# A mixture-of-experts kernel whose largest slots travel through memory in the expert stage in place of at the end of routing

## The chip, the cores and the metric

The kernel runs on one core of one Trainium2 chip. The metric is device time in microseconds (us), of which each run has one; a kernel's figure is the median of its runs. A difference of about 0.3% is what the runs of this kernel can tell from no change. The engines are TensorE (PE), which multiplies, VectorE (DVE), ScalarE (ACT), GpSimd (POOL), which here issues gathers and scatters by index, and SyncE (SP), which here issues most of the other transfers.

## What is computed

Two transformer layers on 2048 tokens (4 sequences of 512) of width 256. Each layer adds an attention and a feed-forward block, both applied to the same layer norm. In the second layer the feed-forward block is a mixture of 64 experts:

```python
x = L0_attn_x
xn = _layernorm(x, axis=-1)
x = x + _L0_attn_ref(xn, ...) + _L0_ffn_ref(xn, ...)
xn = _layernorm(x, axis=-1)
x = x + _L1_attn_ref(xn, ...) + _L1_ffn_ref(xn, ...)

# in _L1_ffn_ref: 8 of 64 experts for each token
topk_idx = jax.lax.top_k(tmp, TOP_K)[1]
topk_w = jnp.take_along_axis(scores, topk_idx, axis=1)
topk_w = topk_w / (topk_w.sum(-1, keepdims=True) + 1e-20) * SCALE
w_full = w_full.at[jnp.arange(T)[:, None], topk_idx].add(topk_w)

def step(out, ws):
    wg, wu, wd, we = ws
    inter = jax.nn.silu(x @ wg.T) * (x @ wu.T)
    return (out + inter @ wd.T * we[:, None], None)
```

The second layer's attention runs over the batch of 4 sequences for each position, so it is small, and VectorE does it beside the experts.

## The kernel before

The program is a row of stages. Each is a block in which every engine has its own list of instructions, and an engine goes into the next stage only when all engines are through with this one (a barrier; its instructions carry the line of the stage's `with ctx`, L1158 or L1496). `layer0` and `layer1_front` take the first 620 us. The two stages of this case are `layer1_routing` and `layer1_experts`.

**Routing.** VectorE picks 8 experts for each token and gives each of the 16384 pairs of token and expert a slot. Slots are ordered by expert, each expert's share is padded to a multiple of 64 (`SEG`), and 128 slots make a block; there are 160 blocks (`NBLK`). One-hot products on TensorE invert this map. VectorE turns the result into `inv` (which token's row a slot takes, L1413) and `dst` (to which row of the memory tensor `y8` its result goes, L1419). GpSimd gathers the rows of blocks 0 and 1 as soon as `inv` is there (`ring.gather`, L189). SP loads experts 0 to 7 into the ring of 16 weight slots (`ring.load`, L183 and L185) and moves the tables of segments (`segments`, `segments_f`) from a column of 128 partitions into rows, through memory. ScalarE ends with a table load and a one-element activation (L1291).

**The largest slots.** The last stage wants to read 3 of each token's 8 results (`EARLY_ROWS`) before all are computed, and so has to know how many scatters must have landed. The slots of a token are sorted, `v8[:, :, TOPK - EARLY_ROWS]` is the largest that matters, and a reduce over the token tiles gives `latest`, one number on each of 128 partitions (L1382). SP stores this column to the memory tensor `latest` in pieces of 4 bytes (L1249), waits, and loads it back as one row on one partition (L1252). VectorE waits for the row (`be_moved` 128), takes its maximum and makes of it, in three further operations on one element, the semaphore value `scattered` (L1424 to L1428).

**Experts.** The blocks are pipelined over all engines. For block `j` GpSimd has gathered the rows into one of 8 buffers (blocks 2 to 9 at the start of this stage, L189, later ones when a buffer is free); TensorE transposes them (`e_ps_xT`, L1814) and VectorE copies them (`e_xT`, L1711); TensorE multiplies by gate and up weights (`e_ps_gu`, L1827), once for each half of 64 slots; ScalarE takes the silu (`e_sg`), VectorE multiplies (`e_h`, the gate, L1728), TensorE transposes (`e_ps_hT`, L1839), VectorE copies (`e_hT`), TensorE multiplies by the down weights (`e_ps_y`, L1850), ScalarE scales (`e_y`) and GpSimd scatters the rows into `y8` (L1633). TensorE takes the down product of block `j - 2` behind the gate and up product of block `j`. VectorE adds one step of the attention behind its work of each block (`attention(*part(j))`); block 100 has a step of the kind `k == 7`, the product `e_prod` at L1771. SP loads experts 8 to 63, each load once the last but one has landed (`landed(e - 1)`) and, from expert 16 on, once the slot is free. Behind all loads SP reads `scattered`, waits for so many scatters and for 12 results of the attention (`y1_ready`), and loads the early rows into `qkv1` (L1603). At the end SP loads the other rows tile by tile (L1613), VectorE adds up the even tiles (L1552), TensorE the odd ones (L1897).

Of the kernel before, what the change touches and what calls it, by code (L numbers as in the profile page):

```python
# [21 lines left out]
P = 128  # L22
# [1132 lines left out]
def layer1_routing(nc, t, late, ring, logits, xT, qkv1, seg_expert, expert_f, inv, dst, last, scattered):  # L1155

    ctx = ExitStack()
    with ctx:  # L1158
# [44 lines left out]
        spare = hi[:, :, :].rearrange("p x c -> p (x c)")  # L1203
        latest_row, latest, bound = spare[0:1, 0:P], spare[:, P:P + 1], spare[0:1, P + 1:P + 2]
# [19 lines left out]
        @block.sync  # L1224
        def _(sp):
            sp.wait_ge(zeroed, 1)
            sp.dma_start(t["rows"][TOK:TOK + P, :], zeros[:, :]).then_inc(cleared, 16)
            sp.wait_ge(w_ready, NT)
            sp.dma_start(t["rows"][0:TOK, D:ROW].rearrange("(n p) e -> p n e", p=P), w[:, :, :])\
              .then_inc(w_out, 16)  # L1230
            for e in range(ring.FIRST):
                ring.load(sp, t, e)

            sp.wait_ge(be_ready, 1)
            for r in range(2):
# [58 lines left out]
        def _(dve):  # L1294
# [87 lines left out]
            V.tensor_reduce(latest[:, :], v8[:, :, TOPK - EARLY_ROWS], AX.X, ALU.max).then_inc(pos_ready, 1)  # L1382
# [24 lines left out]
            for k in range(1, EIGHT):  # L1407
# [84 lines left out]
def layer1_experts(nc, t, ident, late, ring, x_sb, qkv1, seg_expert, expert_f, inv, dst, last, scattered):  # L1492
# [3 lines left out]
    with ctx:  # L1496
        NS, NW, NY, NQ = ring.NS, ring.NW, SCATTERS, 4
        LEAD, NF = 2, 5
        PAIRS = B * (B + 1) // 2
# [15 lines left out]
        mx = sbuf(ctx, nc, "e_mx", [P, H1])  # L1515
        y1 = sbuf(ctx, nc, "e_y1", [P, D])
# [22 lines left out]
        (early_in, summed, x_done_a, x_done_b, stored) = sems(  # L1539
            ctx, nc, "e_early_in", "e_summed", "e_x_done_a", "e_x_done_b", "e_stored")  # L1540
        y8_in = sems(ctx, nc, *(f"e_y8_in{f}" for f in range(NF)))

# [4 lines left out]
        def add_up(eng, E, i, ch, done):  # L1547

            f = i % NF
            eng.wait_ge(y8_in[f], (i // NF + 1) * 16)  # L1550
# [3 lines left out]
            if i in EARLY_TILES:  # L1554
                fold(EARLY_ROWS, qkv1[:, i, :])
                fold(1, y8[:, f, 4 * D:5 * D])
# [26 lines left out]
        def _(sp):  # L1583
# [6 lines left out]
            for e in range(ring.FIRST, NE):  # L1590
# [4 lines left out]
                landed(e - 1)  # L1595
            landed(NE - 1)

            first_rows = sp.value_load(scattered[0:1, 0:1], min_val=16, max_val=NBLK // NY * 16)
            for b in range(NY):
                sp.wait_ge(y_out[b], first_rows)  # L1600
            sp.wait_ge(y1_ready, EARLY_BATCHES * B)
            for i in EARLY_TILES:
                sp.dma_start(qkv1[:, i, :].rearrange("p (k d) -> p k d", d=D), rows8[i, :, LATER:TOPK, :])\  # L1603
# [101 lines left out]
        def _(dve):  # L1705
# [92 lines left out]
            dve.wait_ge(early_in, len(EARLY_TILES) * 16)  # L1798
# [9 lines left out]
        def _(pe):  # L1808
# [78 lines left out]
            pe.wait_ge(early_in, len(EARLY_TILES) * 16)  # L1887
            for i in range(1, NT, 2):
                f = i % NF
                pe.wait_ge(y8_in[f], (i // NF + 1) * 16)  # L1890
                if i // 2 >= 2:
                    pe.wait_ge(x_done_b, i // 2 - 1)
                for k in range(TOPK):
                    row = y8[:, f, k * D:(k + 1) * D]
                    if i in EARLY_TILES and k >= LATER:
                        row = qkv1[:, i, (k - LATER) * D:(k - LATER + 1) * D]
# [5 lines left out]
def kernel_program(nc, t):  # L1902
    ctx = ExitStack()
    with ctx:
# [12 lines left out]
        scattered = sbuf(ctx, nc, "scattered", [1, 1], I32)  # L1917
        layer1_front(nc, t, x_sb, yn, ident, late, ring.early_xT, ring.early_logits, qkv1)
        layer1_routing(nc, t, late, ring, ring.early_logits, ring.early_xT, qkv1, seg_expert, expert_f, inv, dst, last, scattered)
        layer1_experts(nc, t, ident, late, ring, x_sb, qkv1, seg_expert, expert_f, inv, dst, last, scattered)  # L1920
# [73 lines left out]
```

## Time and profile before

| | us |
|---|---|
| median of 3 runs | 1294.45 |
| lowest and highest run | 1294.40, 1297.47 |
| the profiled execution | 1291.48 |
| its span, first to last instruction | 1289.7 |

The span's own busy times, and the page's chain of work that ended last:

```profile
PE 1139.6 (88%) x7654; PEld 660.2 (51%) x7654; DVE 707.7 (55%) x2601; ACT 645.5 (50%) x1340; POOL 453.6 (35%) x525
PE 22%; issue 7%; another core or an unknown queue 6%; ACT 4%; DVE 3%; ACTq 2%; DMA 2%; DVEq 0%; POOL 0%; SPq 0%; POOLq 0%
```

The first line gives busy time, share of the span and number of instructions for each engine (PEld is TensorE's loading of weights, which overlaps its products). Engines whose name ends in q are the sequencers that issue for them; their times aren't in the busy times. A timeline row has the start, the duration, the engine, the line, the operation and `out<-in`, and in brackets how long the engine was idle before it and what ended that. The granted clock of TensorE is given as a share of 2.4 GHz.

### The profile page before, as it was taken

To read this page: it belongs to the slowest core of one execution; us is meant where nothing else is said; L and a number is where in the kernel's file an instruction comes from. 1 tells how busy PE (TensorE), PEld (TensorE's weight loads), DVE (VectorE), ACT (ScalarE), POOL (GpSimd) and SP (SyncE) were. 2 spreads that over 40 slices of the span, in tenths; PEclk is the share of its full clock that TensorE was granted. 3 is DMA by queue.
4 is the path that set the end of the run, shared out by engine and by line. 5 is a ranking of instruction groups with operands and counts; after the bars stand their busy time and mean duration, and the time that the engine had idled before them with its cause. 6 is when DMAs were issued, how large, how long until landed. Compare 5 with 4: busy or idle time off the path is not lost. (4 is left out here: it accounts for less than half of the span.)

```text
span 1289.7 us, 25449 instructions
## 1 busy us (share of the span) xinstructions
PE 1139.6 (88%) x7654; PEld 660.2 (51%) x7654; DVE 707.7 (55%) x2601; ACT 645.5 (50%) x1340; POOL 453.6 (35%) x525
## 2 busy tenths in 40 slices
PE   6679999999999999977974898988898889889967
PEld 3355666666666666455542444444444444444446
DVE  6576565666666666222882544454455455454536
ACT  4215454555555454634362565556555655565520
POOL 3333222222210000022003565565555555555520
PEclk9899999999999999999886999999999999999989
DMA  7401121121112110110066436526364334646248
GB/s 233 82 10 29 32 43 28 29 47 29 28 28 49 20 25 16 51 34 33 8 154 161 133 105 197 169 88 185 108 202 137 125 105 156 206 155 230 83 167 301
DMA packets 81682, 129.67 MB, mean 101 GB/s; under 512 B 32777, under 2 KB 53002, under 8 KB 81035
## 3 DMA queue, kind: packets, MB, share of 16 engines
q1 hardware_dynamic: 61576, 76.94, 21.2%
q0 software_dynamic: 15360, 47.21, 11.6%
q10 hardware_dynamic: 4616, 3.91, 1.0%
q8 instruction: 68, 1.11, 0.4%
q14 instruction: 62, 0.50, 0.1%
HBM read 97.57 MB, written 30.05 MB: 99 GB/s over the span
## 5 line engine op out<-in xcount | busy, mean ns | idle before, releaser
L684 DVE CUSTOM_DVE_ANT_0 a_masked<-a_ps_s,a_mask 128x512 bf16<-128x512 f32 (+3 forms) x512 | 230.0, 488 | 157.6 <-PE a_ps_s L843 153.8
L600 ACT ACTIVATE a_probs<-a_ps_e 128x512 f32<-128x512 f32 (+1 forms) x384 | 187.9, 526 | 120.1 <-PE a_ps_e L863 119.0
L1827 PE MATMUL e_ps_gu<-e_w_gu,e_xT 128*64 x640 | 227.3, 478 | 0.7 <-DVE e_xT L1711 0.7
L1827 PE MATMUL e_ps_gu<-e_s_gu,e_xT 128*64 128x352 f32 x640 | 227.3, 478 | 0.0
L1633 POOL DMA_INDIRECT y<-e_y,dst x160 | 160.4, 1002 | 185.4 <-ACT e_y L1657 81.2
L1850 PE MATMUL e_ps_y<-e_w_d,e_hT 88*64 x640 | 169.8, 388 | 52.8 <-DVE e_hT L1736 37.7
L189 POOL DMA_INDIRECT yn<-rows,inv x160 | 158.3, 989 | 123.8 <-DVE inv L1413 61.4
L1850 PE MATMUL e_ps_y<-e_s_d,e_hT 88*64 88x256 f32 x640 | 170.2, 388 | 0.0
L1728 DVE TENSOR_TENSOR e_h<-e_sg,e_ps_gu 128x176 f32<-128x176 f32 x160 | 54.0, 338 | 211.2 <-ACT e_sg L1648 120.7
L1850 PEld LDWEIGHTS e_ps_y<-e_w_d,e_hT 88*64 88x64 f32 x640 | 81.7, 137 | 148.1 <-issue 124.5
L860 PE MATMUL a_ps_e<-a_qT,a_kT 75*128 75x512 bf16 (+3 forms) x512 | 140.8, 303 | 2.1 <-ACT a_probs L600 1.8
L843 PE MATMUL a_ps_s<-a_kT,a_qT 72*128 72x512 bf16 (+3 forms) x512 | 130.9, 300 | 11.7 <-DVE a_headmax L684 11.4
L1666 ACT ACTIVATE e_s_gu<-e_w_gu 128x704 f32 x160 | 125.2, 783 | 11.6 <-SPq L1586 11.5
L919 PE MATMUL a_ps_f<-a_xnT,a_w_gu 128*128 128x256 f32 x512 | 125.5, 388 | 5.6 <-DVE a_hT L709 3.2
L1648 ACT ACTIVATE e_sg<-e_ps_gu 128x176 f32<-128x176 f32 x160 | 50.0, 312 | 153.1 <-remote 107.1
L1827 PEld LDWEIGHTS e_ps_gu<-e_w_gu,e_xT 128*64 128x64 f32 x640 | 75.4, 138 | 83.2 <-issue 83.2
L1657 ACT ACTIVATE e_y<-e_ps_y,e_weight 128x256 f32<-128x256 f32 x160 | 75.4, 471 | 76.0 <-PE e_ps_y L1850 63.3
L863 PE MATMUL a_ps_e<-a_causal,a_identb 128*128 128x128 bf16 x512 | 112.3, 220 | 0.0
L919 PEld LDWEIGHTS a_ps_f<-a_xnT,a_w_gu 128*128 128x128 f32 x512 | 93.6, 192 | 22.8 <-DVE a_hT L709 10.8
L456 POOL CAST a_m_parts<-a_negmaxT 32x128 bf16<-32x128 f32 x16 | 4.5, 279 | 275.6 <-DVE a_negmaxT L727 155.0
L1671 ACT ACTIVATE e_s_d<-e_w_d 88x512 f32 x160 | 98.9, 618 | 0.0
L1711 DVE COPY e_xT<-e_ps_xT 128x256 f32<-128x256 f32 x160 | 67.7, 423 | 49.8 <-PE e_ps_xT L1814 42.4
(235 smaller groups left out, 1902.6 us busy)
## 6 DMA issues: line engine op xcount, KB each, us to landing
e_w_gu<-e_gu SPq DMA_DIRECT2D x64, 352.0 KB
e_w_d<-e_down SPq DMA_DIRECT2D x64, 176.0 KB
a_qT<-qk_parts SPq DMA_DIRECT2D x48, 192.0 KB
e_w_gu<-y SPq DMA_DIRECT2D x12, 640.0 KB, 6.5
qkv<-y SPq DMA_DIRECT2D x12, 384.0 KB
qk_parts<-a_stage SPq DMA_DIRECT2D x16, 256.0 KB, 2.6
e_w_gu<-y SPq DMA_DIRECT2D x4, 1024.0 KB, 7.0
yn<-rows,inv POOLq DMA_INDIRECT x160
```

What stands on the lines that cost most here:

```text
L189: eng.indirect_dma_start(self.x[:, j % self.NS, :], None, t["rows"], bass.IndirectOffsetOnAxis(inv[:, j:j + 1], 0)).then_inc(self.x_in[j % ...
L600: nc.scalar.activation(probs[:, i % HKV, UCOL[u]:UCOL[u + 1]], ps_e[:, (i * 3 + u) % 2, 0:w], ACT.Exp, scale=SCALE0).then_inc(exp_done, 1)
L684: ins = V.tensor_tensor_reduce(masked[:, n % 2, c:c + w], ps_s[:, n % 2, c:c + w], mask[:, T - w:T], 1.0, -3e38, ALU.add, ALU.max, headmax ...
L843: ins = nc.tensor.matmul(ps_s[:, x % 2, c:c + (a + 1) * P], qT[0:MROW, n % NQ, g, a * P:(a + 1) * P], kT[0:MROW, b % 2, g, 0:(a + 1) * P], ...
L860: nc.tensor.matmul(ps_e[:, x % 2, c:c + T - a * P], kT[:, b % 2, g, a * P:(a + 1) * P], qT[:, n % NQ, g, a * P:T], start=True, stop=False, ...
L863: ins = nc.tensor.matmul(ps_e[:, x % 2, c:c + P], identb[:, :], causal[:, :], start=False, stop=True, skip_group_check=True)
L919: ins = nc.tensor.matmul(ps_f[:, w * HALF:(w + 1) * HALF], w_gu[:, k, w, i * P:(i + 1) * P], xnT[:, n % NX, k, :], start=(k == 0), stop=(k ...
L1633: pool.indirect_dma_start(t["y8"], bass.IndirectOffsetOnAxis(dst[:, j:j + 1], 0), y[:, j % NY, :], None).then_inc(y_out[j % NY], 16)
L1666: nc.scalar.activation(s_gu[:, j % 2].rearrange("p k i -> p (k i)"), w_gu[:, bass.ds(expert & (NW - 1), 1), :, :].rearrange("p a k i -> p ...
L1671: nc.scalar.activation(s_d[:, j % 2].rearrange("p k d -> p (k d)"), w_d[0:HI1, bass.ds(expert & (NW - 1), 1), :, :].rearrange("p a k d -> ...
L1827: ins = nc.tensor.matmul(ps_gu[r * SEG:(r + 1) * SEG, j % 2, 0:2 * INTER1], xT[:, j % 2, k * P + r * SEG:k * P + (r + 1) * SEG], w.rearran ...
L1850: ins = nc.tensor.matmul(ps_y[r * SEG:(r + 1) * SEG, 0:D], hT[:, j % 2, k * P + r * SEG:k * P + (r + 1) * SEG], w.rearrange("p a d -> p (a ...
```

## The change

The store of `latest`, the load back and the four operations leave the routing stage. The column now stays in a tile of its own, `latest_slot`, into the expert stage. There SP stores it behind load 9 (`e == ring.FIRST + 1`), and behind load 15 (`e == NW - 1`) waits for the store and loads the row into an unused part of `seg_expert`. VectorE waits for the row behind its attention step of block 100 and does the four operations there. SP reads `scattered` after its wait for `y1_ready`, not before. The semaphore `early_in` is gone: the store, the load back and the early rows count on the first semaphore of the last part's tiles (`y8_in[0]`), so VectorE and TensorE wait for the early rows and the first tile together. A new tile `e_bound` of 4 bytes lies ahead of `e_y1` and `e_yT`. The slices `early8` and `LATER - 4` are what `qkv1[:, i, :]` and 1 were, with `EARLY_ROWS` = 3.

```diff
 def layer1_routing(...)
         @block.sync
             sp.wait_ge(be_moved, 96)
-
-            sp.wait_ge(pos_ready, 2)
-            sp.dma_start(t["latest"].rearrange("(p a) -> p a", a=1), latest[:, :],
-                         allow_slow_non_contiguous=True).then_inc(be_moved, 16)
-            sp.wait_ge(be_moved, 112)
-            sp.dma_start(latest_row[:, :], t["latest"].rearrange("(a p) -> a p", a=1)).then_inc(be_moved, 16)
-            sp.wait_ge(be_moved, 128)
         @block.vector
-            V.tensor_reduce(latest[:, :], v8[:, :, TOPK - EARLY_ROWS], AX.X, ALU.max).then_inc(pos_ready, 1)
+            ch.did(V.tensor_reduce(latest[:, :], v8[:, :, TOPK - EARLY_ROWS], AX.X, ALU.max))
...
-            dve.wait_ge(be_moved, 128)
-            ch.step(V.tensor_reduce(bound[:, :], latest_row[:, :], AX.X, ALU.max))
-            ch.step(V.tensor_scalar(bound[:, :], bound[:, :], -1.0 - CHOSEN - (SCATTERS * P - 1) / 2,
-                                    1.0 / (SCATTERS * P), ALU.add, ALU.mult))
-            ch.step(V.tensor_scalar(bound[:, :], bound[:, :], 2.0 ** 23, None, ALU.add))
-            ch.step(V.tensor_scalar(scattered[:, :], bound[:, :], 1.0 - 2.0 ** 23, 16.0, ALU.add, ALU.mult))
 def layer1_experts(...)
+        FIRST_ROWS_AT = 100
+        bound = sbuf(ctx, nc, "e_bound", [1, 1])
+        early8 = qkv1[:, :, 3 * D - EARLY_ROWS * D:3 * D]
+        spare = seg_expert[0:1, 3 * P:4 * P].bitcast(F32)
+        scattered = seg_expert[0:1, 3 * P - 1:3 * P]
+        early_in, EARLY_COUNT = y8_in[0], 32 + len(EARLY_TILES) * 16
+
+        def landed_y8(i):
+
+            return y8_in[i % NF], (i // NF + 1) * 16 + (0 if i % NF else EARLY_COUNT)
         @block.sync
                 ring.load(sp, t, e)
                 landed(e - 1)
+                if e == ring.FIRST + 1:
+                    sp.dma_start(t["latest"].rearrange("(p a) -> p a", a=1), latest[:, :],
+                                 allow_slow_non_contiguous=True).then_inc(early_in, 16)
+                if e == NW - 1:
+                    sp.wait_ge(early_in, 16)
+                    sp.dma_start(spare, t["latest"].rearrange("(a p) -> a p", a=1)).then_inc(early_in, 16)
             landed(NE - 1)
-            first_rows = sp.value_load(scattered[0:1, 0:1], min_val=16, max_val=NBLK // NY * 16)
+            sp.wait_ge(y1_ready, EARLY_BATCHES * B)
+            first_rows = sp.value_load(scattered, min_val=16, max_val=NBLK // NY * 16)
             for b in range(NY):
                 sp.wait_ge(y_out[b], first_rows)
-            sp.wait_ge(y1_ready, EARLY_BATCHES * B)
         @block.vector
                 if j < NBLK:
                     attention(*part(j))
-            dve.wait_ge(early_in, len(EARLY_TILES) * 16)
+                if j == FIRST_ROWS_AT:
+
+                    dve.wait_ge(early_in, 32)
+                    ch.step(V.tensor_reduce(bound[:, :], spare, AX.X, ALU.max))
+                    ch.step(V.tensor_scalar(bound[:, :], bound[:, :], -1.0 - CHOSEN - (SCATTERS * P - 1) / 2,
+                                            1.0 / (SCATTERS * P), ALU.add, ALU.mult))
+                    ch.step(V.tensor_scalar(bound[:, :], bound[:, :], 2.0 ** 23, None, ALU.add))
+                    ch.step(V.tensor_scalar(scattered, bound[:, :], 1.0 - 2.0 ** 23, 16.0, ALU.add, ALU.mult))
+            dve.wait_ge(early_in, EARLY_COUNT + 16)
         @block.tensor
-            pe.wait_ge(early_in, len(EARLY_TILES) * 16)
+            pe.wait_ge(early_in, EARLY_COUNT + 16)
             for i in range(1, NT, 2):
                 f = i % NF
-                pe.wait_ge(y8_in[f], (i // NF + 1) * 16)
+                pe.wait_ge(*landed_y8(i))
```

## Rows read from the trace of the kernel before

**Rows 1.** Waits in 670 to 705 us: waiter, releaser, total, times, longest.

```profile
DVE d_hi L1424 <- DMA d_hi<-latest: 11.4, 1, 11.4
```

**Rows 2.** Timeline, 676 to 695 us: the stages' border.

```profile
677.10 0.35 SPq L1249 DMA_DIRECT2D latest<-d_hi  x1
...
677.73 0.95 POOL L189 DMA_INDIRECT yn<-rows,inv  x1 [0.30 <-issue]
678.90 0.20 ACT L1291 ACTIVATE d_warm<-l_bias 128x1 f32<-128x1 f32 x1
684.97 0.24 SPq L1252 DMA_DIRECT2D d_hi<-latest  x1
687.73 0.27 DVE L1424 TENSOR_REDUCE d_hi<-d_hi 1x1 f32<-1x128 f32 x1 [11.37 <-DMA d_hi<-latest]
...
688.39 0.14 DVE L1428 TENSOR_SCALAR scattered<-d_hi 1x1 int32<-1x1 f32 x1
...
689.09 0.66 PE L1814 MATMUL e_ps_xT<-ident_sb,yn 128*128 128x128 f32 x2 [12.35 <-PEq L1158]
...
689.69 0.94 POOL L189 DMA_INDIRECT yn<-rows,inv  x1 [11.01 <-POOLq L1158]
...
690.93 0.94 POOL L189 DMA_INDIRECT yn<-rows,inv  x1 [0.30 <-issue]
...
694.00 0.34 SPq L183 DMA_DIRECT2D e_w_gu<-e_gu  x1
...
694.29 0.29 PEld L1814 LDWEIGHTS e_ps_xT<-ident_sb,yn 128*128 128x128 f32 x2 [1.08 <-DMA yn<-rows,inv]
```

**Rows 3.** The chain that ended last, 640 to 760 us: start, duration, what.

```profile
690.93 5.79 DMA yn<-rows,inv
...
703.92 0.62 PE e_ps_xT L1814 x2
```

**Rows 4.** DMA queues in 678 to 679, 678.5 to 679, 680.5 to 685.5 us: packets, MB, share.

```profile
q0 software_dynamic: 47, 0.16, 55.9%
...
q1 hardware_dynamic: 119, 0.00, 13.4%
...
DMA packets 21, 0.05 MB, mean 10 GB/s; under 512 B 11, under 2 KB 11, under 8 KB 21
```

**Rows 5.** DMA packets in 666 to 668 us, and SP's timeline around them.

```profile
DMA packets 791, 0.12 MB, mean 60 GB/s; under 512 B 736, under 2 KB 736, under 8 KB 791
...
654.70 3.05 SPq L1238 DMA_DIRECT2D segments_f<-d_be  x1
673.62 0.25 SPq L1241 DMA_DIRECT2D seg_expert<-segments  x1
```

**Rows 6.** Gates of L1728 up to 1038.90 us; timeline, 1038.9 to 1043.4 us, block 100.

```profile
694.00:1038.90 344.90, 34.10 (x101) 0.98 0.48 149
...
1038.98 0.68 DVE L1771 TENSOR_TENSOR e_prod<-qkv,e_e 128x512 f32<-128x512 f32 x1
...
1040.22 0.34 DVE L1728 TENSOR_TENSOR e_h<-e_sg,e_ps_gu 128x176 f32<-128x176 f32 x1 [0.56 <-DVE e_prod L1771]
...
1043.31 0.23 PEld L1839 LDWEIGHTS e_ps_hT<-ident_sb,e_h 128*88 128x88 f32 x2
```

**Rows 7.** Timeline, 1248 to 1251 us: the first two tiles of rows.

```profile
1248.57 0.96 DVE L1552 TENSOR_TENSOR e_w_gu<-e_w_gu,qkv 128x768 f32<-128x768 f32 x1 [8.88 <-DMA e_w_gu<-y]
...
1250.41 1.19 PE L1897 MATMUL e_ps_gu<-e_w_gu,ident_sb 128*128 128x256 f32 x2 [9.49 <-DMA e_w_gu<-y]
```

**Rows 8.** Stretches: length, busy PE, PEld, DVE, ACT, POOL; clock; DMA share; GB/s.

```profile
676.74:681.50 4.76, 0.00 (x0) 0.00 (x0) 0.00 (x0) 2.30 (x3) 1.64 (x2) 1.00 0.66 58
681.50:689.06 7.56, 0.00 (x0) 0.00 (x1) 0.70 (x4) 0.00 (x0) 0.00 (x0) 0.50 0.05 7
689.06:695.00 5.94, 4.57 (x16) 1.74 (x18) 1.29 (x5) 2.06 (x4) 4.09 (x5) 0.50 0.73 223
...
701.00:709.00 8.00, 7.05 (x28) 3.19 (x28) 3.26 (x13) 2.46 (x6) 1.97 (x2) 0.57 0.73 217
```

More of the change, by code:

```diff
@@ L1152, in _, with layer1_routing @@
             router(NT - 1)
-def layer1_routing(nc, t, late, ring, logits, xT, qkv1, seg_expert, expert_f, inv, dst, last, scattered):
+def layer1_routing(nc, t, late, ring, logits, xT, qkv1, seg_expert, expert_f, inv, dst, last, latest):
     ctx = ExitStack()
@@ L1202, in layer1_routing @@
         none = sbuf(ctx, nc, "d_none", [P, P], FP16)
-        spare = hi[:, :, :].rearrange("p x c -> p (x c)")
-        latest_row, latest, bound = spare[0:1, 0:P], spare[:, P:P + 1], spare[0:1, P + 1:P + 2]
         ps_inv = psum(ctx, nc, "d_ps_inv", [P, 4, 512])
@@ L1489, in _, with layer1_experts @@
                 qkv(n, 1)
-def layer1_experts(nc, t, ident, late, ring, x_sb, qkv1, seg_expert, expert_f, inv, dst, last, scattered):
+def layer1_experts(nc, t, ident, late, ring, x_sb, qkv1, seg_expert, expert_f, inv, dst, last, latest):
     ctx = ExitStack()
@@ L1538, in layer1_experts @@
         rows8 = t["y8"][0:TOK * TOPK].rearrange("(i p k) d -> i p k d", p=P, k=TOPK)
-        (early_in, summed, x_done_a, x_done_b, stored) = sems(
-            ctx, nc, "e_early_in", "e_summed", "e_x_done_a", "e_x_done_b", "e_stored")
+        early8 = qkv1[:, :, 3 * D - EARLY_ROWS * D:3 * D]
+        spare = seg_expert[0:1, 3 * P:4 * P].bitcast(F32)
+        scattered = seg_expert[0:1, 3 * P - 1:3 * P]
+        (summed, x_done_a, x_done_b, stored) = sems(
+            ctx, nc, "e_summed", "e_x_done_a", "e_x_done_b", "e_stored")
         y8_in = sems(ctx, nc, *(f"e_y8_in{f}" for f in range(NF)))
+        early_in, EARLY_COUNT = y8_in[0], 32 + len(EARLY_TILES) * 16
+        def landed_y8(i):
+            return y8_in[i % NF], (i // NF + 1) * 16 + (0 if i % NF else EARLY_COUNT)
         def done_of(i):
@@ L1549, in add_up @@
             f = i % NF
-            eng.wait_ge(y8_in[f], (i // NF + 1) * 16)
+            eng.wait_ge(*landed_y8(i))
             def fold(n, other):
@@ L1554, in add_up @@
             if i in EARLY_TILES:
-                fold(EARLY_ROWS, qkv1[:, i, :])
-                fold(1, y8[:, f, 4 * D:5 * D])
+                fold(EARLY_ROWS, early8[:, i, :])
+                fold(LATER - 4, y8[:, f, 4 * D:LATER * D])
             else:
@@ L1595, in _ @@
                 landed(e - 1)
+                if e == ring.FIRST + 1:
[4 more added lines that the diff above has]
+                    sp.dma_start(spare, t["latest"].rearrange("(a p) -> a p", a=1)).then_inc(early_in, 16)
             landed(NE - 1)
-            first_rows = sp.value_load(scattered[0:1, 0:1], min_val=16, max_val=NBLK // NY * 16)
+            sp.wait_ge(y1_ready, EARLY_BATCHES * B)
+            first_rows = sp.value_load(scattered, min_val=16, max_val=NBLK // NY * 16)
             for b in range(NY):
                 sp.wait_ge(y_out[b], first_rows)
-            sp.wait_ge(y1_ready, EARLY_BATCHES * B)
             for i in EARLY_TILES:
-                sp.dma_start(qkv1[:, i, :].rearrange("p (k d) -> p k d", d=D), rows8[i, :, LATER:TOPK, :])\
+                sp.dma_start(early8[:, i, :].rearrange("p (k d) -> p k d", d=D), rows8[i, :, LATER:TOPK, :])\
                   .then_inc(early_in, 16)
@@ L1895, in _ @@
                     if i in EARLY_TILES and k >= LATER:
-                        row = qkv1[:, i, (k - LATER) * D:(k - LATER + 1) * D]
+                        row = early8[:, i, (k - LATER) * D:(k - LATER + 1) * D]
                     ins = nc.tensor.matmul(ps_gu[:, i // 2 % 2, 0:D], ident[:, :], row,
@@ L1916, in kernel_program @@
         last = sbuf(ctx, nc, "last", [1, NE], I32)
-        scattered = sbuf(ctx, nc, "scattered", [1, 1], I32)
+        latest = sbuf(ctx, nc, "latest_slot", [P, 1])
         layer1_front(nc, t, x_sb, yn, ident, late, ring.early_xT, ring.early_logits, qkv1)
-        layer1_routing(nc, t, late, ring, ring.early_logits, ring.early_xT, qkv1, seg_expert, expert_f, inv, dst, last, scattered)
-        layer1_experts(nc, t, ident, late, ring, x_sb, qkv1, seg_expert, expert_f, inv, dst, last, scattered)
+        layer1_routing(nc, t, late, ring, ring.early_logits, ring.early_xT, qkv1, seg_expert, expert_f, inv, dst, last, latest)
+        layer1_experts(nc, t, ident, late, ring, x_sb, qkv1, seg_expert, expert_f, inv, dst, last, latest)
 def constants():
```

## The prediction

> **What bounds the kernel now.** The page comes first: TensorE is the busiest engine, and in the expert stage the others work for it, so a stretch without TensorE is time lost. The edit sits where the routing stage ends and the expert stage begins; the waits from 670 to 705 us [rows 1] show VectorE idle for 11.4 us there, on a DMA that writes `d_hi` from `latest`. The timeline of the same stretch [rows 2] gives the order, and the reader should follow the engines to the barrier between the stages one by one. VectorE ends `dst` at 687.73 - 11.37 = 676.36 and has nothing until 687.73; its last operation ends at 688.39 + 0.14 = 688.53, and TensorE starts the expert stage at 689.09. So one chain sets the end of routing: the store of `latest` (issued 677.10), its landing, the load back (issued 684.97, used from 687.73) and four operations on one element.
>
> **What the others have done by then** [rows 2]. SP is past its wait for `expert_f` at 677.10, where it issues the store. GpSimd's second gather ends at 677.73 + 0.95 = 678.68. ScalarE ends its warm-up at 678.90 + 0.20 = 679.10. TensorE has done nothing since 676.74 [rows 8]. Without the chain ScalarE is last.
>
> **Part 1: the chain leaves the end of routing.** Out of it go two DMAs, their waits on SP, one wait and four operations on VectorE. The last arrival moves from 688.53 to 679.10: 9.43 us. What follows the barrier keeps its distance to it: TensorE 689.09 - 688.53 = 0.56 us, GpSimd 689.69 - 688.53 = 1.16 us [rows 2]. The chain of work that ended last [rows 3] goes from the barrier over GpSimd's gathers for blocks 2 and 3 to a landing at 690.93 + 5.79 = 696.72 and on into TensorE, so it moves by the same 9.43 us. The blocks follow no clock of their own, so the shift is kept to the end unless something below gives it back. Term: -9.4 us.
>
> **Part 2: gathers 0 and 1 lose their cover.** Now they have 10 us to land before TensorE wants them. Gather 2 ends on GpSimd at 689.69 + 0.94 = 690.63, and TensorE, which waits for it, starts at 694.29: 3.66 us. Gather 3 ends at 691.87 and lands at 696.72: 4.85 us. Both have two expert loads beside them [rows 2, 3]. Gather 0 ends at 677.73 - 0.30 = 677.43, gather 1 at 678.68; by 3.66 us they land at 681.1 and 682.3, by 4.85 us at 682.3 and 683.5. Shifted by 9.43, TensorE wants them at 689.09 - 9.43 = 679.7 and, one transpose and copy later, at about 680.9. So it starts up to 2.6 us late. It then has under 4.6 us of work (689.06 to 695.00, at the low clock [rows 8]) before it needs gather 3, at 696.72 - 9.43 = 687.3: 682.3 + 4.6 = 686.9. Hidden; I take 0, with 0 to 2.6 us as bounds.
>
> **Part 3: the store of `latest` in its new place.** It is issued after expert load 9, once load 8 has landed. That is where load 10 goes out now, at 694.00 [rows 2], so the store is issued at about 684.6, and load 10 behind it on SP and in queue 1 about 0.4 us later. SP's wait for it comes after load 15, when everything up to load 14 has landed, so SP isn't held. The cost is another one. The store is 128 pieces of 4 bytes. Of its packets 119 run in 678.5 to 679, and it lands at 684.97. Queue 0, which moved gather 0 (0.16 MB) in 678 to 679, puts only 21 packets, at 10 GB/s, into 680.5 to 685.5: the tail of gather 1, issued just behind the store [rows 4]. There is a second case: `segments` and `segments_f`, also in 4 byte pieces, have their last packets in 666 to 668, and SP can go on only at 673.62 [rows 5]. I read both as: such a store is confirmed some 5.5 us after its last packet, and transfers of other queues on the same DMA engines stall meanwhile. In the new place gather 3 and later and load 10 are what can stall. Load 10 doesn't matter, since experts 0 to 8 are there. Gather 3 does. It lands at 687.3 and its last packets move about 1 us before, at 686.3. The store's packets come at 684.6 + 1.4 = 686.0 at the earliest (677.10 to 678.5 now), and behind what is left of load 9. That is a near miss. If gather 3 is caught, it lands at about 686.5 + 5.5 = 692.0 and costs 4.7 us. If it isn't, gather 4 is caught, but that is wanted only at 703.92 - 9.43 = 694.5 [rows 3]. I take 0, the time order being for it, with 0 to 4.7 us as bounds.
>
> The Trainium skill (DMA: Bandwidth & Descriptors, Queues, rings and completion order) says that the increment of a semaphore lands only after every earlier write of that DMA engine, of all its queues. By that rule alone the store was confirmed late because gather 1 was slow; it would delay nobody, and the term would be 0 with no bound above. The second case speaks against it as the whole story, for no gather was under way there.
>
> **Part 4: the load back and the four operations.** The load (684.97 to 687.73 with its landing) goes behind load 15, and nobody wants it before block 100. VectorE has made 101 gates (`e_h`) by 1038.90, so its step of block 100 is the one at 1038.98 [rows 6]. The four operations take 688.53 - 687.73 = 0.80 us there. Queued behind them is the gate of block 101, with 0.56 us of idle time in front of it, so it is pushed by 0.3 us, and the copies of `e_xT` and `e_hT` behind it by no more. TensorE transposes this `e_h` at 1043.31; the gate ends at 1040.56: 2.7 us of cover. Term 0; 0.8 us without the cover.
>
> **Part 5: what else is touched.** The reduce into `latest` is the same operation on another tile. SP reads `scattered` after its wait for `y1_ready` in place of before; both stand behind all 64 expert loads, so 0. At the end VectorE and TensorE wait for the first tile of rows together with the early ones. VectorE waited for it anyway (until 1248.57), and TensorE starts at 1250.41, later than that [rows 7]: 0. `e_bound` moves the tiles behind it by 4 bytes; no row prices that, and I put it at 0 with the 0.3 us of block 100 as bound on either side.
>
> **Part 6: TensorE's clock.** It was granted 1.00 (2.4 GHz) until 681.50, 4.8 us after the last matmul, 0.50 (1.2 GHz) from there to 695.00, and 0.57 on average from 701 to 709 [rows 8]. After the change TensorE restarts at about 681, so the first dip may stay away, but what it slows is waiting for gather 3 anyway. The second dip lies on the path: 7.05 us of matmuls at 0.57 would be 4.0 us at 1.00, so it costs 3.0 us. It may go, or another may come with a changed rhythm: -3.0 to +3.0, taken as 0.
>
> **The sum.** -9.43 + 0 (gathers 0, 1) + 0 (store) + 0 (block 100) + 0 (clock) = -9.4 us. The profiled execution took 1291.48 us (span 1289.7), so its like would take 1282.1. The median of the runs before is 1294.45, 3.0 us above it, and what is compared is medians: 1294.45 - 9.4 = 1285.0 us.
>
> **Rivals.** (a) Gather 3 is caught by the store: 9.4 - 4.7 = 4.7 us gained, 1289.7 us. For it speaks the crawl of gather 1; against it load 9 ahead of the store and gather 3's head start. (b) The forecast with the second clock dip gone: 9.4 + 3.0 = 12.4, 1282.0 us. For it speaks that TensorE's long rest at the low clock goes; against it that the idle time just before 701 stays. (c) Nothing moves: the barrier, or code behind it, is late for another reason. Only the crowd of waiting engines speaks for it; against it each engine's last work is seen, at 679.10 or before. 1294.5 us. (d) Slower. One mechanism: the store takes as long behind loads as `segments_f` did, 654.70 to 673.62 = 18.9 us from its issue [rows 5], and holds gather 3 all that time: 684.6 + 18.9 = 703.5 against 687.3 costs 16.2 us, net +6.8, 1301.3 us. From a landing of gather 3 after 696.7 on it is slower. Against it: `segments_f` had most of eight loads ahead, the store has at most one.
>
> **Chances.** Forecast 0.54 (1282.5 to 1287.5 around 1285.0), (a) 0.26 (1288 to 1292), (b) 0.10, (c) 0.06, (d) 0.04. A measurement of this kernel tells 0.3%, 3.9 us, from no change. Faster by more: 0.54 + 0.10 + two thirds of (a) = 0.82. Within: the rest of (a) and (c) = 0.14. Slower 0.04. For 8 in 10 the range takes the forecast, (b) but for its end, and two thirds of (a), up to 1290.5: 1280.0 to 1290.5.
>
> **What would show it.** Right: VectorE has no wait behind `dst`; ScalarE's warm-up is the last work before TensorE's first transpose, 0.5 to 3 us before it; TensorE's wait for gather 3 ends about 9.4 us earlier; the four operations stand behind block 100's step, and TensorE's next transpose of `e_h` doesn't wait for VectorE. Queue 0 crawls for about 5 us after the store's packets if my reading of them holds. Rival (a): gather 3's wait ends only 4 to 5 us earlier. The forecast is wrong if a gather, from block 3 on, holds TensorE longer than now, or if a shift that is there at block 10 is gone at block 150.

## The result and the profile after

| | before | after |
|---|---|---|
| median, 8 runs each, us | 1297.18 | 1285.91 |
| lowest and highest, us | 1291.44, 1300.21 | 1284.40, 1290.04 |
| profiled execution: time, span | 1291.48, 1289.7 | 1285.63, 1283.8 |

The ratio is 0.9924, with a 95% interval of 0.9903 to 0.9946: 9.9 us of 1297.18, between 7.0 and 12.6; the two medians as they stand differ by 11.3. Run again beside other kernels (`after_again`), the changed kernel came to 0.9939 (0.9913 to 0.9965).

The changed kernel's timeline at the border of the stages, which answers to [rows 2]. Columns are as there.

```profile
677.88 0.38 DVE L1404 SCALAR_TENSOR_TENSOR inv<-d_is_pad,l_ids,d_token 128x160 uint32<-128x160 f32 x1
...
679.05 0.33 DVE L1410 SCALAR_TENSOR_TENSOR dst<-d_row,d_pad_row 128x160 uint32<-128x160 f32 x1
679.20 1.24 POOL L189 DMA_INDIRECT yn<-rows,inv  x1 [62.06 <-DVE inv L1404]
...
680.74 0.95 POOL L189 DMA_INDIRECT yn<-rows,inv  x1 [0.30 <-issue]
681.91 0.20 ACT L1282 ACTIVATE d_warm<-l_bias 128x1 f32<-128x1 f32 x1
684.06 0.66 PE L1821 MATMUL e_ps_xT<-ident_sb,yn 128*128 128x128 f32 x2 [4.31 <-PEq L1158]
...
684.65 0.94 POOL L189 DMA_INDIRECT yn<-rows,inv  x1 [2.96 <-POOLq L1158]
...
688.91 0.34 SPq L1590 DMA_DIRECT2D latest<-latest_slot  x1
```

VectorE has nothing behind `dst`: the wait of [rows 1] is gone. But the two spans can't be laid on each other by their clocks. `inv`, which the edit doesn't touch, begins at 677.88, where it began at 674.87 before:

```profile
674.87 0.38 DVE L1413 SCALAR_TENSOR_TENSOR inv<-d_is_pad,l_ids,d_token 128x160 uint32<-128x160 f32 x1
```

Of these 3.0 us, 1.2 are seen at 200 us already, in stages whose code is the same, and 2.35 at the reduce into `latest` (645.85 before, 648.20 after), which is the first operation that the edit touches. The rest is no effect of the edit that could be told: from this reduce to `inv` the kernels below take 28.1 to 29.7 us, though the code between the two is the same in nearly all of them. So I count from `inv` on, in this kernel and in all others below. "The barrier opens" is read from TensorE's first transpose of the expert stage:

| us after `inv` begins | before | after | moved |
|---|---|---|---|
| TensorE's first transpose of the expert stage | 14.22 | 6.18 | 8.0 |
| gate (`e_h`) of block 0 | 19.88 | 11.84 | 8.0 |
| gate of block 5 | 39.78 | 28.10 | 11.7 |
| gate of block 50 | 192.44 | 182.49 | 10.0 |
| gate of block 99 | 359.09 | 348.35 | 10.7 |
| gate of block 159, the last | 561.51 | 552.47 | 9.0 |
| end of the span | 614.83 | 605.92 | 8.9 |

The border gives 8.0 us, the first blocks some 3.6 more, the long stage gives back 2.7, and 8.9 us are left, which with the 3.0 us of drift makes the 5.9 us between the spans. Only the first three rows can be leaned on. In `after_again`, with the same code, they are 6.14, 11.81 and 28.05, within 0.1 us of this execution; but the gate of block 99 comes at 351.87 there, 3.5 us later than here. So a difference of 2 or 3 us deep in the long stage can't be told from what one execution differs from the next.

### The profile page after: what moved, and what is told of

Same layout as the page of the kernel before. It is cut to its first block and busy times, and to the rows that moved or that the text cites. A ratio compares the mean times of both kernels' runs of the same rounds, so it can differ in the third digit from the quotient of the medians.

```text
span 1283.8 us, 25448 instructions
## 1 busy us (share of the span) xinstructions
PE 1143.0 (89%) x7654; PEld 660.1 (51%) x7654; DVE 707.9 (55%) x2601; ACT 645.6 (50%) x1340; POOL 456.3 (36%) x525
## 5 line engine op out<-in xcount | busy, mean ns | idle before, releaser
L1834 PE MATMUL e_ps_gu<-e_w_gu,e_xT 128*64 x640 | 230.3, 483 | 0.7 <-DVE e_xT L1710 0.7
L1834 PE MATMUL e_ps_gu<-e_s_gu,e_xT 128*64 128x352 f32 x640 | 230.3, 483 | 0.0
L1632 POOL DMA_INDIRECT y<-e_y,dst x160 | 163.0, 1019 | 181.8 <-ACT e_y L1656 85.0
```

Of the source, the lines that this page charges most:

```text
L1632: pool.indirect_dma_start(t["y8"], bass.IndirectOffsetOnAxis(dst[:, j:j + 1], 0), y[:, j % NY, :], None).then_inc(y_out[j % NY], 16)
L1834: ins = nc.tensor.matmul(ps_gu[r * SEG:(r + 1) * SEG, j % 2, 0:2 * INTER1], xT[:, j % 2, k * P + r * SEG:k * P + (r + 1) * SEG], w.rearran ...
```

## The experiments

Each compares with the kernel before on the same chip, timed in 5 rounds or, where no ratio is given, in one profiled execution. The edits are against the changed kernel where nothing else is said. On the chip of the second set (three stores, row store, late store, row made on TensorE) the kernel before was slower, 1302.15 us against 1294.18 and 1294.48 in the other two, so only ratios, and times counted from `inv` near the border, go across the sets.

### No transport at all

```diff
-                if e == ring.FIRST + 1:
-                    sp.dma_start(t["latest"]..., latest[:, :], ...).then_inc(early_in, 16)
-                if e == NW - 1:
-                    ...
-                if j == FIRST_ROWS_AT:
-                    ...
-            first_rows = sp.value_load(scattered, ...)
             for b in range(NY):
-                sp.wait_ge(y_out[b], first_rows)
+                sp.wait_ge(y_out[b], 256)
```

> Nothing of the largest slots travels: no store, no load back, no operations at block 100; SP waits for a constant number of scatters (256 on each of the eight semaphores, worked out beforehand from the routing) in place of the computed one. Theory A (the stalled DMA engines cost nothing that TensorE sees): time as the changed kernel's, ratio to before 0.990 to 0.993; the packets of the gathers in the 8 us behind load 9 move at more than 100 GB/s. Theory B (the stalls reach TensorE through gather 3 or a later one): 4 to 5 us less than the changed kernel, ratio 0.988 or 0.989.

Beside the two transfers, VectorE's four operations at block 100 are left out. Measured: 0.994 (0.9913 to 0.9967), so what the changed kernel still does for the slots costs nothing that these runs can tell. But the DMA engines do feel it. The same 8 us, from 16 us after `inv` on, in the changed kernel and in this one (length; busy time and count of PE, PEld, DVE, ACT, POOL; granted clock, DMA share, GB/s), the changed kernel first:

```profile
693.88:701.88 8.00, 7.63 (x48) 3.69 (x48) 3.96 (x17) 4.13 (x9) 2.44 (x3) 0.88 0.79 64
```

```profile
691.90:699.90 8.00, 5.14 (x28) 2.52 (x28) 3.58 (x15) 3.85 (x8) 2.35 (x3) 0.79 0.95 282
```

With the store 64 GB/s move, without it 282. `after_again`, the changed kernel in another execution, has the crawl for 6 us, from 15 to 21 us after `inv`:

```profile
689.99:695.99 6.00, 3.50 (x26) 1.63 (x26) 2.67 (x11) 2.73 (x6) 1.26 (x3) 1.00 0.72 75
```

So its length isn't fixed: here 6 us, above about 8. TensorE is busy for 7.63 of 8 us in the first fence, so it isn't starved there; but that it is busier than in the second (5.14) is no effect of the store, for in the same stretch of `after_again` it is 5.50. Theory A holds: the rate is above 100 GB/s, and the ratio lies nearer to its range (0.990 to 0.993) than to that of B, though the interval excludes neither a small cost nor a small gain.

### The store put back, with nobody waiting for it

```diff
 # routing, SP, behind its wait for expert_f
+            sp.wait_ge(pos_ready, 2)
+            sp.dma_start(t["latest"].rearrange("(p a) -> p a", a=1), latest[:, :],
+                         allow_slow_non_contiguous=True).then_inc(ring.latest_in, 16)
 # experts, SP
-                if e == ring.FIRST + 1:
-                    sp.dma_start(...)
```

> The store goes back to the end of routing, but nobody waits for it there; load back and operations stay in the expert stage. Theory A (a store in 4 byte pieces stalls the DMA engines for 5.5 us and more, and what is queued behind it with them): the barrier opens as in the changed kernel, about 6.2 us after inv, but gather 1 lands only about 10 us after inv, so TensorE transposes block 1 about 4 us later than the changed kernel does, counted from inv; ratio to before about 0.996. Theory B (a store's confirmation only waits for earlier writes and delays nobody): block 1 is transposed 1.3 us after block 0, ratio 0.992.

The timeline of this kernel at the border, with `inv` at 680.53:

```profile
680.45 0.34 SPq L1248 DMA_DIRECT2D latest<-latest_slot  x1
...
683.39 0.95 POOL L190 DMA_INDIRECT yn<-rows,inv  x1 [0.30 <-issue]
684.56 0.20 ACT L1287 ACTIVATE d_warm<-l_bias 128x1 f32<-128x1 f32 x1
...
692.00 0.66 PE L1823 MATMUL e_ps_xT<-ident_sb,yn 128*128 128x128 f32 x2 [9.60 <-PEq L1159]
...
692.60 0.94 POOL L190 DMA_INDIRECT yn<-rows,inv  x1 [8.25 <-POOLq L1159]
```

And its stretch from 4 to 10 us after `inv`, in the columns of the last two fences:

```profile
684.53:690.53 6.00, 0.00 (x0) 0.00 (x0) 0.00 (x0) 0.22 (x2) 0.00 (x0) 0.71 0.39 29
```

Every engine's last work before the barrier is over at 684.76, nobody waits for the store, and yet TensorE starts at 692.00: 11.47 us after `inv` at 680.53, against 6.18 in the changed kernel. In the last fence the gathers trickle at 29 GB/s; their last packets fall between 10 and 11 us after `inv`. The ratio is 1.0005 (0.9979 to 1.0031): nearly all of the gain is gone. I had expected 0.996; the 2.75 us that the border is still ahead of the kernel before would be 0.998, at the edge of the interval. (The last gate of this one profile, 554.15 us after `inv`, would promise far more: it can't be trusted for such sums.) This refutes that a store delays nobody. In one respect it went otherwise than I expected: I foresaw block 1's transpose to be late and the barrier to be on time, and it is the barrier that is late, with GpSimd's queue the one that has gathers under way. That SP is held there by its own store, still unconfirmed, is a rival that no run here excludes for this kernel and for the one with two such stores below; what speaks for GpSimd stands in the next section.

### Who is last at the barrier

```diff
 # e_one_gather
-    NS, NW, SOON, FIRST = 8, 16, 2, 8
+    NS, NW, SOON, FIRST = 8, 16, 1, 8
 # e_no_table
-            nc.scalar.activation(warm[:, :], late.bias[:, 0:1], ACT.Silu)
```

> Gather 1 moves behind the barrier. In the changed kernel TensorE's first transpose of the expert stage begins 6.18 us after inv begins and 1.95 us after ScalarE's last work. Theory G (GpSimd goes through the barrier only when its gathers are out, one gather costing 1.2 us): the first transpose begins about 5 us after inv. Theory S (ScalarE's table load is last): still 6.2 us. Theory C (the code behind the barrier): still 6.2 us.

> ScalarE's table load and one-element activation are left out at the end of routing, so the table load falls to the first silu of the expert stage. Theory S (ScalarE is last at the barrier): the first transpose begins about 1.5 us earlier, 4.7 us after inv. Theories G (GpSimd last) and C (code behind the barrier): still 6.2 us.

With one gather (first fence) and without the table load (second):

```profile
683.47 0.20 ACT L1282 ACTIVATE d_warm<-l_bias 128x1 f32<-128x1 f32 x1
...
684.36 0.41 PE L1821 MATMUL e_ps_xT<-ident_sb,yn 128*128 128x128 f32 x2 [3.06 <-PEq L1158]
...
684.96 0.96 POOL L189 DMA_INDIRECT yn<-rows,inv  x1 [2.96 <-POOLq L1158]
...
689.68 0.69 PE L1821 MATMUL e_ps_xT<-ident_sb,yn 128*128 128x128 f32 x2 [4.91 <-DMA yn<-rows,inv]
```

```profile
680.45 0.96 POOL L189 DMA_INDIRECT yn<-rows,inv  x1 [0.30 <-issue]
683.79 0.41 PE L1820 MATMUL e_ps_xT<-ident_sb,yn 128*128 128x128 f32 x2 [4.33 <-PEq L1158]
```

One gather less in the routing stage opens the barrier 4.92 us after `inv` (684.36 - 679.44) in place of 6.18. Without the table load it opens at 6.20 (683.79 - 677.59), as before. So ScalarE, which I had taken, isn't last in the changed kernel, and GpSimd is. With one gather the two may be level: ScalarE's last work ends 4.23 us after `inv` (683.67 - 679.44), and in the kernel before the first transpose followed the last arrival by 0.56 us, so the gather may cost a little more than the 1.26 us seen.

These two runs don't tell issuing a gather (1.25 us each) from its being out, for both are taken away at once. The packets do. Over five kernels the last packets of GpSimd's queue fall into the half microsecond that begins, counted from `inv`, at 4.0 (one gather), 5.0 (changed kernel), 5.0 (row store in the whole chain, below), 10.5 (store put back) and 13.0 (two stores, below), and TensorE's first transpose comes at 4.92, 6.18, 6.16, 11.47 and 13.89, each time 0.4 to 1.2 us behind them. GpSimd had issued its last gather by 3.8 us after `inv` in all five. So the barrier follows the landing. In the kernel before, the last packets fall at 10.0 to 10.5 and the transpose at 14.22: there the gathers too are late, behind the chain that is later still. The gain of one gather less is no use by itself: gather 1 then starts late, and TensorE waits 4.91 us for it.

### More stores, another store, another place

```diff
 # e_three_stores, on top of e_nothing
+                if ring.FIRST + 1 <= e <= ring.FIRST + 3:
+                    n = e - ring.FIRST - 1
+                    sp.dma_start(t["latest"][n * P:(n + 1) * P].rearrange("(p a) -> p a", a=1), latest[:, :], ...)
 # e_row_store, on top of e_nothing
+                if e == ring.FIRST + 1:
+                    sp.dma_start(t["latest"].rearrange("(a p) -> a p", a=1), seg_expert[0:1, 0:P].bitcast(F32))
 # e_store_later
-                if e == ring.FIRST + 1:
+                if e == 24:
-                if e == NW - 1:
+                if e == 32:
```

> As the kernel in which nothing travels (SP waits for the constant 256), but with three stores of the column in 4 byte pieces, behind loads 9, 10 and 11. Theory A (each such store stalls the DMA engines some 5.5 us or more): gathers 4 to 9 land late enough to hold TensorE, blocks 3 to 8 come 5 to 12 us later than in the changed kernel, ratio to before 0.995 to 1.001. Theory B (a store delays nobody): as with no store, 0.990 to 0.993, and the packets behind the stores move at more than 100 GB/s.

> As the kernel in which nothing travels (SP waits for the constant 256), but with one store of 512 bytes in one piece (a row of another tile) where the changed kernel stores the column. Theory A (the 4 byte pieces are what stalls): no crawl, the gathers' packets in the 8 us behind it move at more than 100 GB/s. Theory B (any store to memory between the loads does): the same crawl as in the changed kernel, at 15 to 70 GB/s.

> The store goes behind load 24 and the load back behind load 32. Theory A (4 byte pieces stall the DMA engines wherever they are): no crawl at the start of the stage, and one of the same kind, 5 us and more with less than 100 GB/s, behind load 24; TensorE isn't held, since gathers run several blocks ahead there. Theory B (the crawl belongs to the start of the stage, with its eight gathers and loads at once): the crawl stays at the start.

SP's timeline with three stores, then the 8 us from 16 us after `inv` on with the row store, then, for the late store (issued at 797.20, behind load 24), one stretch that is nearly all ahead of it and two behind it:

```profile
687.43 0.34 SPq L1591 DMA_DIRECT2D latest<-latest_slot  x1
687.81 0.43 SPq L183 DMA_DIRECT2D e_w_gu<-e_gu  x1
688.28 1.82 SPq L185 DMA_DIRECT2D e_w_d<-e_down  x1
698.14 0.34 SPq L1591 DMA_DIRECT2D latest<-latest_slot  x1
```

```profile
694.46:702.46 8.00, 4.34 (x22) 2.01 (x20) 3.17 (x13) 3.42 (x7) 1.60 (x3) 0.79 0.79 255
```

```profile
790.00:798.00 8.00, 7.68 (x51) 3.49 (x49) 3.35 (x12) 4.56 (x10) 4.80 (x5) 1.00 0.85 259
...
802.00:803.00 1.00, 1.00 (x11) 0.47 (x9) 0.96 (x2) 0.32 (x1) 0.70 (x2) 1.00 0.87 39
...
804.00:806.00 2.00, 1.65 (x15) 0.65 (x10) 1.66 (x3) 0.82 (x2) 1.69 (x2) 1.00 0.99 63
```

With three stores SP waits from 690.10 to 698.14 before it can go on, where without a store it issues a load about every 3 us; with the changed kernel's one store the like wait is 6.1 us (693.56 to 699.71). With one piece of 512 bytes there is no crawl (255 GB/s). With the store behind load 24 the crawl is there, at 39 to 70 GB/s for some 6 us, and TensorE is busy through it. So the crawl belongs to the 4 byte pieces, and to no place. The ratio of three stores is 0.9944 (0.9918 to 0.997): I had expected 0.995 or more under theory A, with blocks 3 to 8 late by 5 to 12 us. The gate of block 5 comes 34.32 us after `inv`, where it comes at 31.01 and 32.58 in the two kernels without such stores on the same chip (row made on TensorE, row store), and the one of block 10 at 50.18 against 47.27 and 48.74: 1.4 to 3.3 us late. So even so much stalling hardly reaches TensorE.

### The row made on TensorE

```diff
+                if j == FIRST_ROWS_AT - 4:
+                    nc.tensor.transpose(ps_yT[0:1, D:D + P], latest[:, :], ident[:, :]).then_inc(row_ready, 1)
...
-                    dve.wait_ge(early_in, 32)
-                    ch.step(V.tensor_reduce(bound[:, :], spare, AX.X, ALU.max))
+                    dve.wait_ge(row_ready, 1)
+                    ch.step(V.tensor_reduce(bound[:, :], ps_yT[0:1, D:D + P], AX.X, ALU.max))
```

> The column becomes a row on TensorE: one transpose at block 96 into unused columns of the PSUM bank of e_ps_yT, read there by VectorE's reduce at block 100; no store, no load back. Theory A (the stalls cost nothing that TensorE sees): as the changed kernel, ratio to before 0.990 to 0.993. Theory B (they do): 4 to 5 us less, 0.988 or 0.989. Under both it isn't slower than the changed kernel: one transpose of about 0.3 us is added among 160 blocks.

0.9926 (0.9896 to 0.9956): as the changed kernel, with no DMA for the slots at all. It doesn't beat it.

### The changed kernel again, beside the last set

> The changed kernel once more, beside the others of this set on the same chip: ratio to before 0.990 to 0.995.

0.9939 (0.9913 to 0.9965): the gain is there in another set of runs too.

### Must the chain leave the routing stage?

```diff
 # e_chain_with_row_store, on top of the kernel before
-            sp.dma_start(t["latest"].rearrange("(p a) -> p a", a=1), latest[:, :],
-                         allow_slow_non_contiguous=True).then_inc(be_moved, 16)
+            sp.dma_start(t["latest"].rearrange("(a p) -> a p", a=1),
+                         seg_expert[0:1, 0:P].bitcast(F32)).then_inc(be_moved, 16)
 # e_store_with_segments, on top of the kernel before: the same store, issued right behind segments_f
-            sp.wait_ge(be_moved, 48)
+            sp.wait_ge(pos_ready, 2)
+            sp.dma_start(t["latest"]..., latest[:, :], ...).then_inc(be_moved, 16)
+            sp.wait_ge(be_moved, 64)
+            sp.dma_start(latest_row[:, :], ...).then_inc(be_moved, 16)
 # e_two_stores_at_end, on top of e_store_at_end_of_routing
+            for n in range(2):
```

> The kernel before with its whole chain at the end of routing, but with a store of 512 bytes in one piece (a row of another tile) in place of the column, so that the number that is worked out is not that of the slots, and SP waits for the constant 256 in its place. Theory A (the 4 byte pieces are what is slow): the store is confirmed in 2 to 3 us in place of 7.9, VectorE's last operation ends 8 to 9 us after inv in place of 13.7, and the first transpose begins 9 us after inv in place of 14.2. Theory B (any store and load back costs this): nothing moves.

> The kernel before, with the store of the column issued together with segments and segments_f, some 20 us earlier, and the load back with theirs; all of it and the four operations stay in the routing stage. Theory A (the gain comes from having no store in 4 byte pieces, and no wait for one, near the border of the stages; where the rest is done doesn't matter): VectorE doesn't wait, its four operations end about 2.4 us after inv, the first transpose begins 6.2 us after inv, and the ratio is that of the changed kernel, 0.990 to 0.995. Theory B (the expert stage is the only place where it is hidden): the wait stays in part, ratio 0.996 to 1.000.

> As the kernel with the unwaited store at the end of routing, with two such stores one behind the other. Theory A1 (a stall has a length of its own for each piece): the tail of gather 1 and the barrier with it come 4 to 6 us later than with one store, the first transpose 16 to 17 us after inv. Theory A2 (the length is that of one confirmation, however many pieces are on the way): within 1.5 us of one store, 11.5 to 13 us after inv.

The timeline of the whole chain, with a row in place of the column:

```profile
677.49 0.39 DVE L1413 SCALAR_TENSOR_TENSOR inv<-d_is_pad,l_ids,d_token 128x160 uint32<-128x160 f32 x1
...
678.64 0.24 SPq L1249 DMA_DIRECT2D latest<-seg_expert  x1
...
679.73 0.22 SPq L1252 DMA_DIRECT2D d_hi<-latest  x1
...
681.67 0.14 DVE L1428 TENSOR_SCALAR scattered<-d_hi 1x1 int32<-1x1 f32 x1
...
683.65 0.41 PE L1813 MATMUL e_ps_xT<-ident_sb,yn 128*128 128x128 f32 x2 [4.29 <-PEq L1158]
```

The number that it makes isn't that of the slots, and SP waits for the constant 256. The store is on its way for 1.1 us (678.64 to 679.73) where the column took 7.9. VectorE is through 4.3 us after `inv`, and the barrier opens at 6.16, exactly as with the whole chain moved away. I had expected 9. One execution took 1283.96 us, less than any of the 23 of the kernel before on this chip (lowest 1289.99). So the move isn't what helps at the border: the pieces are. With them gone, both the wait and the crawl of the gathers that holds GpSimd are gone.

The store issued early, with `segments`, was a miss for theory A. It isn't free there. Issued at 659.99, behind the pieces of `segments` and `segments_f`, it lets SP go on with the load back only 2.8 us after `inv` (680.24). In the kernel before, SP went on with `seg_expert` 1.3 us before `inv` [rows 5], in the kernel with the store put back 3.5 us before it. So the tables that it is queued with come 4 us later or more, and VectorE waits for them:

```profile
681.52 0.20 ACT L1288 ACTIVATE d_warm<-l_bias 128x1 f32<-128x1 f32 x1
684.24 0.27 DVE L1421 TENSOR_REDUCE d_hi<-d_hi 1x1 f32<-1x128 f32 x1 [5.26 <-DMA expert_f<-segments_f]
```

The wait is for `expert_f`, through the count that it shares. The barrier opens at 8.10 and the ratio is 0.9975 (0.9951 to 0.9999). Two stores at the end open the barrier 13.89 us after `inv` (693.33 - 679.44), 2.4 us more than one. Neither A1 (4 to 6) nor A2 (under 1.5) foretold that; how the stall grows with the number of pieces stays open, and each of the two is one execution.

## Why the prediction was right, and where its steps were not

**The sum** was -9.4 us and 1285.0 us; the median is 1285.91, the ratio says -9.9 (-7.0 to -12.6). Sign and size hold. That 1285.0 is within 1 us of the median is in part luck: it starts from 1294.45, the median of 3 runs before, and with 8 runs that is 1297.18. The one term in the sum was 1.4 us too large, and the 8.0 us that were measured for it lie in the interval by themselves; that something else made up for the rest isn't shown. (In the chances a sum is off by 0.01: 0.54 + 0.10 + two thirds of 0.26 is 0.81.)

**Part 1, the border.** The mechanism is shown: the chain was last, and without it the barrier opens sooner. The size is 8.0 us and not 9.43, and the step that failed is "Without the chain ScalarE is last". I had read GpSimd's last work off the end of its issuing (678.68). It goes through the barrier when its gathers have landed; the runs with one gather and without the table load, and the last packets in five kernels, show it. My sign for this step, ScalarE's warm-up as the last work 0.5 to 3 us before the first transpose, came true (1.95 us) and told nothing: it can't tell ScalarE from a queue whose end isn't on the engine's timeline. Of the 8.0 us, taking away the waits alone gives 2.75 (14.22 to 11.47, store still there), and only the absence of the column's pieces gives the other 5.3 (11.47 to 6.18). The other way round, with the pieces away and the waits kept, all 8.1 are there (14.22 to 6.16). What the pieces do I had not in the sum's reasoning at all, though the crawl of gather 1 stood in [rows 4].

**Part 2, gathers 0 and 1.** I had put their lateness at 0 to 2.6 us behind the barrier. It is in the barrier: 1.4 us of it (9.43 against 8.0), and behind it block 1 is transposed 1.3 us after block 0, with no wait for a gather. The 3.66 and 4.85 us that I took for a gather's landing were too long for these two, which have no loads beside them: in the changed kernel the last packets of gather 1 are through by 683.4, 1.7 us after its issue ends (681.69). And the 3.66 us was an upper bound only. I had read "TensorE, which waits for it, starts at 694.29" off the row of a weight load; TensorE's products before it run to 694.35 in the profile, so gather 2 may have landed well before.

**Part 3, the store.** My reading of the two cases was right, and the rule of the Trainium skill (DMA: Bandwidth & Descriptors, Queues, rings and completion order), that a confirmation waits for the earlier writes of its engine, isn't the whole story: in `e_store_at_end_of_routing` the gathers crawl behind a store that nobody waits for. The stall is longer than my 5.5 us (8 us at 64 GB/s, and 6 us at 75 in `after_again`). Gather 3 wasn't caught, as forecast. The waits at the start of the stage in the changed kernel (waiter, releaser, total, times, longest):

```profile
PE e_ps_xT L1821 <- PEq L1158: 4.3, 1, 4.3
...
PEld e_ps_xT L1821 <- DMA yn<-rows,inv: 3.3, 2, 2.2
```

The longer of the two waits in there, for gather 2, ends at 690.37, and most of the store's pieces move from 690.9 to 691.9, where 119 packets under 512 bytes go, after 39 in the microsecond before. The shorter, for gather 3, is one of TensorE's weight load and hidden: gather 3 didn't gate. TensorE took it at 693.53, straight out of block 1's matmuls, which ran at the low clock: 15.65 us after `inv` against 21.90, which is 6.2 us of shift, less than the 9.4 that I had expected for it. Gather 2 lands 5.7 us after its issue begins here and 4.6 us in the kernel without transport, but 4.6 us too with three stores, of which the first goes out at the same place, and in `after_again`, whose code is the same. So the 1.1 us is a difference between executions and not the store's.

**Part 4, block 100.** Shown, on VectorE's timeline of the changed kernel:

```profile
1031.94 0.68 DVE L1770 TENSOR_TENSOR e_prod<-qkv,e_e 128x512 f32<-128x512 f32 x1
1032.65 0.27 DVE L1800 TENSOR_REDUCE e_bound<-seg_expert 1x1 f32<-1x128 f32 x1
...
1033.31 0.14 DVE L1804 TENSOR_SCALAR seg_expert<-e_bound 1x1 int32<-1x1 f32 x1
1033.49 0.34 DVE L1727 TENSOR_TENSOR e_h<-e_sg,e_ps_gu 128x176 f32<-128x176 f32 x1
```

From 1032.65 to 1033.45 they take 0.80 us, as foreseen, and the gate of block 101 follows 2.67 us after the one of block 100, where it followed after 2.36 in the kernel before, 0.3 us less. But its rhythm around block 100 was another. The kernel without transport has the changed kernel's rhythm there, and not the operations; its gates of blocks 100 and 101:

```profile
1031.58 0.34 DVE L1720 TENSOR_TENSOR e_h<-e_sg,e_ps_gu 128x176 f32<-128x176 f32 x1 [1.55 <-ACT e_sg L1640]
1033.41 0.34 DVE L1720 TENSOR_TENSOR e_h<-e_sg,e_ps_gu 128x176 f32<-128x176 f32 x1
```

They are 1.83 us apart. So the gate is pushed by the whole 0.8 us and not by 0.3, and the cover holds all the same: the gate of block 102 follows the one of block 99 after 11.25 us with the operations and 11.22 without. The term 0 is right. The ratio without them is no better either (0.994).

**Part 5.** Nothing speaks against its zeros: from the last gate to the end of the span it is 53.32 us before and 53.45 after. The 4 bytes of `e_bound` weren't tried by themselves.

**Part 6, the clock.** What rival (b) said of the second dip did come about at the start, though the median isn't at its 1282.0. The changed kernel's stretch at the times of the fourth of [rows 8], and the one before it:

```profile
695.00:701.00 6.00, 5.63 (x39) 2.62 (x36) 3.17 (x13) 2.72 (x6) 1.90 (x2) 0.94 0.75 60
701.00:709.00 8.00, 7.36 (x54) 3.51 (x53) 4.70 (x16) 5.23 (x11) 5.15 (x6) 1.00 0.93 318
```

The first dip stayed (TensorE was granted 0.50 from 684.06 to 695, 1.2 GHz, after 4.3 us without work). The second, 0.57 over 8 us in [rows 8], is gone. From block 0 to block 5 the shift grows by 3.6 us, near the 3.0 priced. But the move of the border isn't what takes the dip away. The kernel without transport, whose border is as early, still has it:

```profile
695.90:697.90 2.00, 2.00 (x10) 1.00 (x12) 1.01 (x4) 1.65 (x3) 1.00 (x1) 0.57 0.83 258
697.90:699.90 2.00, 2.00 (x14) 0.90 (x10) 0.41 (x2) 0.32 (x1) 0.98 (x1) 0.58 1.05 282
```

Its gate of block 5 comes at 29.69, the changed kernel's at 28.10 and 28.05 (`after_again`): 1.6 us that the dip costs it, if nothing else differs. In the 4 us before those rows its TensorE was idle for 2.9 us. In the changed kernel it was hardly idle there (0.4 us), in `after_again` for 2.5 us, and neither has the dip. What decides over it stays open. By block 10 little is left of it: 47.30 us after `inv` without transport, 47.36 and 46.52 in the two profiles of the changed kernel, 57.37 before. What wears off after that, down to 9.0 us at the last gate, is within what two executions of the same code differ by (3.5 us at block 99).

**The other rivals.** (a), gather 3 caught: not seen. (c), nothing moves: refuted by the 8.0 us. (d), a hold of 19 us: the longest seen is three stores' 8 us wait of SP (690.10 to 698.14), and TensorE is hardly held by that.

## What to carry to other kernels

Read the last arrival at a barrier from what each engine waits for there, its transfers included, and not from its last instruction. A column of one number on each of 128 partitions is cheap in bytes and dear in pieces: if it must go through memory, keep it away from transfers that somebody waits for, or make a row of it first (on TensorE, at the cost of one transpose). When a wait for a transfer is taken off a path, ask what the transfer itself does to its neighbours: here it cost more (5.3 us) than the wait alone gave back (2.75).

## What the runs showed of the hardware that I had not expected

- A store of 128 pieces of 4 bytes keeps other transfers of the core, of another queue too, at 29 to 75 GB/s for 6 to 8 us; in the expert stage 255 to 282 GB/s move there without it. The same 512 bytes in one piece do nothing of the kind and are confirmed within 1.1 us in place of 7.9. A second such store right behind adds 2.4 us (one execution).
- GpSimd doesn't get through a barrier while its gathers are on the way: in five kernels TensorE's first transpose comes 0.4 to 1.2 us behind the gathers' last packets. A gather of 128 rows costs some 1.26 us there, and 5.3 us more when they crawl.
